# Attention: the fp16 halves of the probabilities cut by ScalarE and GpSimd and turned by DMA

## The reference, cut to what matters

```python
q = (layernorm(x) @ Wq)                      # per head, 64 wide
k, v = y @ Wkv                               # y: 1601 x 192 context
atten = softmax(einsum('bhid,bhjd->bhij', q, k) * SCALE, axis=-1)
res = einsum('bhij,bhjd->bhid', atten, v)
x = x + res @ Wproj + bproj
```

## Time and profile before

| | us |
|---|---|
| Median of three runs | 3374.56 |
| The profiled execution | 3373.66 |
| Its span, first to last instruction | 3371.6 |
| TensorE busy in the span | 3077.0 (91%) |
| VectorE, ScalarE, GpSimd busy | 2115.1, 1776.3, 941.7 |
| Tile loop of the attention, first score to last `X` addition | 85.4 to 2551.0 |

### The profile page before, as it was taken

One profiled execution on the slowest core, in us unless ns is written; L12 is line 12 of the kernel. 1 busy time (PEld: TensorE's weight loads), 2 busy tenths in 40 slices (PEclk: granted clock), 3 DMA queues, 4 the chain that ended last, 5 costly groups with the idle time before them and its releaser, 6 DMA issues. The chain is left out here.

```text
span 3371.6 us, 72486 instructions
## 1 busy us (share of the span) xinstructions
PE 3077.0 (91%) x27524; PEld 2053.9 (61%) x27524; DVE 2115.1 (63%) x4407; ACT 1776.3 (53%) x3522; POOL 941.7 (28%) x1018
## 2 busy tenths in 40 slices
PE   4999999999999999999999999999996557768998
PEld 3666667666766666676667667666764221145665
DVE  4666566656666665656565665656564659945665
ACT  2545454545455454545454454545453658815665
POOL 2141222222221322222222313222200238825553
PEclk8999999999999999999999999999998779988999
DMA  4111111111111211111111102111002000002111
GB/s 149 35 60 34 47 35 35 35 36 35 35 37 35 60 35 46 35 35 35 36 35 35 44 27 68 33 40 35 16 1 71 0 10 1 1 22 65 55 57 46
DMA packets 70375, 131.29 MB, mean 39 GB/s; under 512 B 6800, under 2 KB 52496, under 8 KB 69744
## 3 DMA queue, kind: packets, MB, share of 16 engines
q1 hardware_dynamic: 70000, 126.23, 12.9%
HBM read 122.02 MB, written 4.19 MB: 37 GB/s over the span
## 5 line engine op out<-in xcount | busy, mean ns | idle before, releaser
L428 PE MATMUL psum<-yT,Q 128*128 128x512 f16 (+1 forms) x5120 | 982.5, 333 | 14.5 <-issue 13.0
L452 PE MATMUL psum<-yN,pT 128*128 128x384 f16 (+1 forms) x3328 | 836.5, 326 | 0.0
L454 PE MATMUL psum<-yN,pT 128*128 128x192 f16 (+1 forms) x3328 | 815.1, 246 | 0.0
L645 DVE TENSOR_TENSOR pT<-psum,pT 128x512 f16<-128x512 f32 (+1 forms) x1024 | 578.6, 587 | 262.8 <-ACT pT L555 248.4
L555 ACT ACTIVATE pT<-psum 128x512 f16<-128x512 f32 (+1 forms) x1024 | 498.7, 514 | 433.0 <-PE psum L440 431.1
L428 PEld LDWEIGHTS psum<-yT,Q 128*128 128x128 f16 x5120 | 448.1, 98 | 384.7 <-issue 18.5
L338 POOL CAST yT<-stage 128x1601 f16<-128x1601 f32 x32 | 48.7, 1522 | 1825.7 <-DVE On L670 1785.5
L633 DVE TENSOR_REDUCE mx<-psum 128x1 f32<-128x1024 f32 (+1 forms) x512 | 481.9, 978 | 50.9 <-PE psum L428 32.2
L440 PE MATMUL psum<-ident,prob 128*128 128x128 f32 (+1 forms) x3328 | 502.2, 277 | 10.9 <-ACT prob L547 10.5
L547 ACT ACTIVATE prob<-psum,nb 128x1601 f32<-128x1601 f32 x256 | 408.6, 1596 | 194.7 <-DVE nb L637 194.7
L440 PEld LDWEIGHTS psum<-ident,prob 128*128 128x128 f32 (+1 forms) x3328 | 362.8, 140 | 150.3 <-DVE pT L645 93.4
(11 more groups left out here) (162 smaller groups left out, 3785.3 us busy)
## 6 DMA issues: line engine op xcount, KB each, us to landing
stage<-in_ctxT SPq DMA_DIRECT2D x32, 800.5 KB, 4.3
stage<-in_ctxT SPq DMA_DIRECT2D x64, 400.2 KB
stage<-in_ctxN SPq DMA_DIRECT2D x32, 672.0 KB, 3.9
wnat<-in_WF SPq DMA_DIRECT2D x32, 512.0 KB, 4.2
stage<-in_ctxN SPq DMA_DIRECT2D x32, 480.0 KB
X<-in_x SPq DMA_DIRECT2D x1, 2048.0 KB, 8.2
Wk<-in_WkS SPq DMA_DIRECT2D x1, 2048.0 KB, 16.4
x_rows<-X SPq DMA_DIRECT2D x1, 2048.0 KB, 8.2
```

The lines of the kernel that those rows point to most:

```text
L428: ins = pe.matmul(psS[:, lo:hi], Q[u][:, q, b, tt * P:(tt + 1) * P], yT[b][:, y, lo:hi], start=(n == 0), stop=(n == 4))
L452: pe.matmul(psO[:, 0:2 * CTX], pT[0][0:k, n, :], yN[b][0:k, n, :], start=(n == 0), stop=False)
L454: ins = pe.matmul(psO[:, 0:CTX], pT[1][0:k, n, :], yN[b][0:k, n, 0:CTX], start=False, stop=(n == JN - 1))
L645: dve.tensor_tensor(pT[1][0:w, lo:hi, :], psT[g % 2][0:w, 0:(hi - lo) * P].rearrange("p (n h) -> p n h", h=P), pT[0][0:w, lo:hi, :], ALU.s ...
```

## The change

The attention's tile loop is rewritten; the arithmetic is the same apart from where the halves are cut.

- The 13 transposes on TensorE, ScalarE's four PSUM copies and VectorE's four subtractions of a tile are gone. ScalarE casts `prob` to fp16 in one instruction (`ph`), GpSimd subtracts it (`pl`), and SyncE issues two DMA transposes per tile, SBUF to SBUF: `ph` to `hT` and `pl` to `lT`, both 128x1664 fp16. `ph` and `pl` have one buffer each, `hT` and `lT` two.
- The gather of a tile is two steps behind its scores (`BEHIND = 2`), `turn_o` three steps behind.
- The loops are unrolled over all 256 tiles. The projection is spread: one batch of nine matmuls in each of the steps `t` = 12 to 15 and, of the pair before, `t` = 0 to 3. It has a PSUM bank of its own.
- The context comes in eight pieces per batch element through three smaller staging buffers, one piece cut and one loaded per tile.

```diff
-        stage = [sb(f"stage{i}", [P, J]) for i in range(2)]
+        JH = 801
+        PIECES, RING = 8, 3
+        stage = [sb(f"stage{i}", [P, JH]) for i in range(RING)]
-        pT = [sb(f"pT{i}", [P, JN, P], F16) for i in range(2)]
+        ph = sb("ph", [P, JN * P], F16)
+        pl = sb("pl", [P, JN * P], F16)
+        hT = [sb(f"hT{i}", [P, JN, P], F16) for i in range(2)]
+        lT = [sb(f"lT{i}", [P, JN, P], F16) for i in range(2)]
...
+        # SyncE
+            for K in range(PIECES + 2):
+                load(K)
+            sp.wait_ge(pad_set, 2)
+            for G in range(NT):
+                if G >= 2:
+                    sp.wait_ge(summed, G - 1)
+                sp.wait_ge(hi_kept, G + 1)
+                sp.dma_start_transpose(hT[G % 2][:, :, :], ph[:, :]).then_inc(hi_turned, 16)
+                sp.wait_ge(lo_kept, G + 1)
+                sp.dma_start_transpose(lT[G % 2][:, :, :], pl[:, :]).then_inc(lo_turned, 16)
+                if G + PIECES + 2 < B * PIECES:
+                    load(G + PIECES + 2)
...
+        # GpSimd
+            for K in range(PIECES + 1):
+                cut(K)
+            for G in range(NT):
+                pool.wait_ge(hi_kept, G + 1)
+                if G:
+                    pool.wait_ge(lo_turned, 16 * G)
+                pool.tensor_tensor(pl[:, 0:J], prob[:, :], ph[:, 0:J], ALU.subtract).then_inc(lo_kept, 1)
+                if G + PIECES + 1 < B * PIECES:
+                    cut(G + PIECES + 1)
...
+            def gather(G):
+                b = G // HP % 2
+                if G:
+                    pe.wait_ge(normed, G)
+                pe.wait_ge(hi_turned, 16 * (G + 1))
+                pe.wait_ge(lo_turned, 16 * (G + 1))
...
+            # TensorE
+            for G in range(NT + BEHIND + 2):
+                p, t = divmod(G, 16)
+                if G < NT:
+                    score(G)
+                if BEHIND + 1 <= G < NT + BEHIND + 1:
+                    turn_o(G - BEHIND - 1)
+                if BEHIND <= G < NT + BEHIND:
+                    gather(G - BEHIND)
+                if t >= 12 and G < NT:
+                    project(p, t - 12)
+                if t < 4 and p:
+                    project(p - 1, t + 4)
+                # t < 2: q_half of the next pair; 2 <= t < 10: qk_group
...
+            def exponentials(G):
+                act.wait_ge(biased, G + 1)
+                if G:
+                    act.wait_ge(lo_kept, G)
+                act.activation(prob[:, :], psS[:, 0:J], ACT.Exp, bias=nb[:, G % 2:G % 2 + 1], scale=SCALE,
+                               accum_out=den[:, G % 4:G % 4 + 1]).then_inc(expd, 1)
+
+            def high(G):
+                act.wait_ge(expd, G + 1)
+                if G:
+                    act.wait_ge(hi_turned, 16 * G)
+                act.activation(ph[:, 0:J], prob[:, :], ACT.Copy).then_inc(hi_kept, 1)
...
+            # ScalarE, each step: exponentials(G), high(G), o_copy(G-3), sum_low(G-2), q_copy or qk_high
+            # VectorE, each step: maximum(G), reciprocal(G), o_low(G-3), normalise(G-2), q_low or qk_low,
+            #                     at t == 4 the addition of the pair before to X
```

More of the change, by code:

```diff
@@ L290, in attention, with place, transfers, loaded_by @@
         x_added = sem("x_added")
-        AHEAD, LO_AHEAD, CTX_AHEAD = 16, 4, 2
-        GROUPS = [(0, 4), (4, 8), (8, 12), (12, 13)]
+        NT = 16 * NPAIR
+        BEHIND = 2
+        def place(G):
+            p, t = divmod(G, 16)
+            b, tt = divmod(t, HP)
+            return p, t, b, tt
+        def transfers(part):
+            return 2 if part in (2, 3) else 1
+        def loaded_by(K):
+            return 16 * sum(transfers(k % PIECES) for k in range(K % RING, K + 1, RING))
+        def half_cols(part):
+            return slice(0, JH) if part % 2 == 0 else slice(JH, J)
@@ L371, in _, with q_half @@
+            for K in range(PIECES + 1):
[7 more added lines that the diff above has]
+                    cut(G + PIECES + 1)
         @block.tensor
         def _(pe):
-            def q_half(pair, half, misc_free):
-                misc_free()
+            def q_half(pair, half):
@@ L395, in qk_group, with score @@
                 ins.then_inc(qk_done, 1)
[L397 to L402, removed]
+            def score(G):
+                p, t, b, tt = place(G)
+                if tt == 0:
+                    pe.wait_ge(piece_cut, PIECES * (G // HP + 1))
+                if t == 0:
+                    pe.wait_ge(qk_lo, HP * (p + 1))
+                if G:
+                    pe.wait_ge(expd, G)
+                for c in range(4):
+                    lo, hi = 512 * c, min(J, 512 * (c + 1))
+                    for n, (q, y) in enumerate([(0, 0), (1, 1), (0, 2), (2, 0), (3, 1)]):
+                        ins = pe.matmul(psS[:, lo:hi], Q[p % 2][:, q, b, tt * P:(tt + 1) * P],
+                                        yT[b][:, y, lo:hi], start=(n == 0), stop=(n == 4))
+                    if c in (1, 3):
+                        ins.then_inc(scored, 1)
@@ new lines, in gather @@
+            def gather(G):
[4 more added lines that the diff above has]
+                pe.wait_ge(lo_turned, 16 * (G + 1))
+                for n in range(JN):
+                    k = P if n < JT else JR
+                    pe.matmul(psO[:, 0:2 * CTX], hT[G % 2][0:k, n, :], yN[b][0:k, n, :], start=(n == 0), stop=False)
+                    ins = pe.matmul(psO[:, 0:CTX], lT[G % 2][0:k, n, :], yN[b][0:k, n, 0:CTX], start=False, stop=(n == JN - 1))
+                ins.then_inc(summed, 1)
@@ new lines, in turn_o, with project @@
+            def turn_o(G):
+                pe.wait_ge(normed, G + 1)
+                if G:
+                    pe.wait_ge(o_kept, G)
+                for k in range(2):
+                    ins = pe.transpose(psT[:, k * P:(k + 1) * P], On[:, k * P:(k + 1) * P], ident[:, :])
+                ins.then_inc(o_turned, 1)
+            def project(p, tt):
+                pe.wait_ge(o_kept, 16 * p + HP + tt + 1)
+                if tt == 0 and p:
+                    pe.wait_ge(x_added, p)
+                for n, k in enumerate((2 * tt, 2 * tt + 1, H + tt)):
+                    for m, (o, w) in enumerate([(0, 0), (0, 1), (1, 0)]):
+                        ins = pe.matmul(psP, OT[:, o, k, :], Wvp[:, w, k, :], start=(tt == 0 and n == m == 0),
+                                        stop=(tt == HP - 1 and n == m == 2))
+                ins.then_inc(projected, 1)
@@ new lines, in _ @@
+                if g:
+                    pe.wait_ge(qk_lo, g)
+                qk_group(g)
+            for G in range(NT + BEHIND + 2):
+                p, t = divmod(G, 16)
+                if G < NT:
[8 more added lines that the diff above has]
+                    project(p - 1, t + 4)
+                if t < 10 and p + 1 < NPAIR:
+                    if t < 2:
+                        if t == 0:
+                            pe.wait_ge(qk_lo, HP * (p + 1))
+                        else:
+                            pe.wait_ge(q_kept, 2 * p + 3)
+                        q_half(p + 1, t)
+                    else:
+                        if t == 2:
+                            pe.wait_ge(q_kept, 2 * p + 4)
+                        else:
+                            pe.wait_ge(qk_lo, HP * (p + 1) + t - 2)
+                        qk_group(t - 2)
@@ new lines, in _ @@
+            q_copy(0)
+            q_copy(1)
+            for g in range(HP):
+                qk_high(g)
+            for G in range(NT + BEHIND + 1):
+                p, t = divmod(G, 16)
+                if G < NT:
+                    exponentials(G)
+                    high(G)
+                if BEHIND + 1 <= G:
+                    o_copy(G - BEHIND - 1)
+                if BEHIND <= G < NT + BEHIND:
+                    sum_low(G - BEHIND)
+                if t < 10 and p + 1 < NPAIR:
+                    if t < 2:
+                        q_copy(2 * p + 2 + t)
+                    else:
+                        qk_high(HP * (p + 1) + t - 2)
@@ new lines, in maximum @@
+            def maximum(G):
+                m = 2 * (G % 2)
+                for n, (lo, hi) in enumerate([(0, 1024), (1024, J)]):
+                    dve.wait_ge(scored, 2 * G + n + 1)
+                    dve.tensor_reduce(mx[:, m + n:m + n + 1], psS[:, lo:hi], AX_X, ALU.max).then_inc(maxed, 1)
+                dve.wait_ge(maxed, 2 * G + 2)
+                dve.tensor_scalar(nb[:, G % 2:G % 2 + 1], mx[:, m:m + 1], mx[:, m + 1:m + 2], -SCALE,
+                                  ALU.max, ALU.mult).then_inc(biased, 1)
@@ new lines, in _ @@
+            dve.memset(ph[:, J:], 0.0).then_inc(pad_set, 1)
+            dve.memset(pl[:, J:], 0.0).then_inc(pad_set, 1)
+            q_low(0)
+            q_low(1)
+            for g in range(HP):
+                qk_low(g)
+            for G in range(NT + BEHIND + 3):
+                p, t = divmod(G, 16)
+                if G < NT:
+                    maximum(G)
```

(13 more changed lines are left out.)

412 lines of the change are left out of this document (107 added, 305 removed).

## The result

The changed kernel takes 2960.56 us (median of four runs, 2959.42 to 2961.37), the kernel before 3375.95 us beside it. The ratio is 0.877, with a 95% interval of 0.875 to 0.878: 415 us less.

The account below looks back on a forecast made before the run. TensorE's own instructions, 98% busy in the tile loop, were taken as the bound. Each tile takes the longest of three loops: 132.6 us a pair, stage 2127 us, 338 less than 2465.6, so 3036 us; range 2940 to 3950.

Parts of the forecast that it names:

- The bound and what goes: Tile loop: TensorE's own instructions bind, 98% busy; 1.55 us a tile of transposes and short waits go from it.
- the 10 us of the last pair: Last pair of the stage: it forms no next queries, so 10 us less than the other pairs.
- What comes: New work per tile: ScalarE's cast 1.50 us, GpSimd's subtraction 3.22, a DMA transpose 4.3 to landing.
- the low bound: DMA transpose priced as a plain transfer of 426 KB: about 3.2 us to landing.
- The high bound of 12.6 us: DMA transpose priced as 1664 packets of 256 bytes at 99 ns each over 16 engines: 12.6 us to landing.
- The loops: Three loops run from tile to tile: `pl` 7.6 us, ScalarE-VectorE queues 7.38 or 8.15, TensorE 6.83 plus additions; the longest counts.
- the `pl` loop: GpSimd's next subtraction waits for the low half's landing: 3.22 + 4.3 + 0.1 of handovers, 7.6 us a tile.
- the chain: ScalarE and VectorE in-order queues, from one exponential to the next: 7.38 us, 8.15 with a `qk_group`.
- The slack: In front of the exponential: GpSimd's subtraction of the tile before is done 0.9 us before VectorE lets the exponential start.
- TensorE as the only bound: Rival, tile loop: each tile takes TensorE's own time, 126.7 us a pair, 2942 us in all; chance 0.08.
- The transposes setting the pace: Rival, tile loop: landing over 6.3 us makes the kernel slower, 3817 us at 8 us, about 6200 at 12.6; chance 0.34.

Follow-up runs that it names:

- e4_dummy: The changed kernel with 13 fp32 transposes of the identity, read by nothing, added on TensorE ahead of each tile's scores: 3290.62 us.
- e6_unroll: The kernel before with its attention loops unrolled on all five engines, nothing else changed: 3346.01 us against 3373.34 beside it.
- e8_nolow: The changed kernel without the low half's transpose and GpSimd's wait for it; the gather reads `hT` in place of `lT`: 2960.70 us.
- e1_order: The changed kernel with ScalarE copying tile G-3's turned output before tile G's exponential, and VectorE doing `o_low` before the reciprocal: 2925.91 us.
- e7_third: The changed kernel with a third transpose per tile, the high half into a spare buffer, and two staging buffers in place of three: 3092.86 us.

## Why the prediction was right, and where it was 75 us off

*The bound and what goes* held. The transposes' time on TensorE was paid out, 330 us by e4_dummy, and 27 more came from the turns of the loop (e6_unroll). No run shows the other 58 us by themselves, but the traces place them. In the order before, with turns between the scores, a tile takes 9.05 or 8.37 us where e4_dummy, with the same work in one block, takes 8.93 or 8.25: 0.12 a tile, some 29 us. A pair takes 152.1 us in e6_unroll and 148.9 in e4_dummy, which leaves about 22 us for the pairs' ends, where the projection stood alone. And the kernel before forms a 17th set of queries that nothing reads. The counts of TensorE's instructions on the two pages differ by 3456: 3328 transposes and 128 matmuls of that set, 9 us by the earlier trace rows. Together that is about 60. The set is one thing that the change took away besides what the section on it names. The forecast had the first two in its comparison of 154.1 with 132.6 us a pair, without naming them, and the third among the 10 us of the last pair.

*What comes* held for the cast and the subtraction. The transpose landed in 3.4 us, where 4.3 was taken and 3.2 was the low bound. The high bound of 12.6 us erred in the price of a packet. The count was nearly right: the queue has 952688 packets in the changed kernel and 518512 in e8_nolow, which is 1696 per transpose against 1664. But one takes 2.2x16/1696 = 0.021 us and not the 0.099 of the mean packet before.

The estimate from the Trainium skill's "DMA: Bandwidth & Descriptors", section "Latency and other measured facts", was 1.6 us of moving, at the 261 GB/s stated there; the 2.2 us worked out above are 194 GB/s. The estimate of 17 us, from the Trainium skill's "VectorE: DVE Perf Modes", section "The three transpose paths", took the time stated there for one block 13 times; 13 blocks in one instruction landed in 3.4 us, so that price can't be multiplied by the number of blocks.

*The loops* were the right ones, and each tile took the longest, but for three tiles: at `t` = 10 and 11 the forecast let the `pl` loop bind and at `t` = 12 TensorE, and it was the chain. The sum was too large by these terms, per pair:

- the chain of ScalarE and VectorE, 7.38 forecast and 7.16 measured, 8.15 and 7.83 with a `qk_group`. Back-to-back instructions of one engine overlap by some 0.1 us in the records: the next start after `o_low`'s and after `normalise`'s is earlier than the sum of durations, and the five handovers of 0.04 were mostly within the durations. Five tiles at 0.32 are 1.6 us.
- `pl`: 7.6 forecast, 3.23+3.4+0.1 = 6.7 with the measured landing, so it binds nowhere. With the chain, 0.9 us in the tiles of 7.16 before the projection.
- the first projection tile goes by the chain (7.16 for 7.85), the next is 7.72: 0.9 us.
- the addition to `X`: 8.16 for 8.57, 0.4; a `q_half` 1.75 us by starts for the 1.95 of its duration, 0.4 in two tiles.

These are 4.2 of the 4.3 us between 132.6 and 128.3, 69 us over 16 pairs. The loop was 73.5 us shorter than forecast; the rest lies at its two ends. The first pair took 120.4 us, since no projection of a pair before it runs in it, and the forecast gave it 132.6 like the others. The end after the last exponential's start at 2120.48 fits: from its end 1.68 later to 2138.6 it is 16.4 us, 16 forecast.

*The slack* in front of the exponential was there in nearly every tile, but in the tiles of 7.16 it was smaller than the 0.9 us forecast. In the tile shown above the subtraction ends at 1079.59 and the bias at 1080.15: 0.56 us. With a `qk_group` it is 1.22. VectorE ended 827.4 us of the waits in front of the exponential and GpSimd the other 29.7 us. The forecast's busy share of about 90% for TensorE doesn't follow from its own sum, in which 126.7 of 132.6 us, 96%, are TensorE's; 99% was measured.

*What was luck.* The transpose had no row, and the landing taken for it was the one term that nothing in the trace tied down. It came out 0.2 us above the low bound. A landing of 5.4 us, 2 more than measured, would by the forecast's own rule have made the `pl` loop 8.7 us, longer than TensorE's time in 14 of a pair's 16 tiles.

*The rivals.* TensorE as the only bound, 2942 us with a chance of 0.08, missed by 19 us, and the measured time lies nearer to it than to the forecast. What the forecast held against it, the written order of ScalarE's and VectorE's work, was the whole of the difference: e1_order takes the copies of `OT` and `o_low` out of the chain and reaches 2926. The transposes setting the pace, the largest rival with 0.34, was a fear of an unknown duration; e7_third shows that this kernel had room for two a tile and not for three.

## What to carry to other kernels

Where one engine is at 98% and is its own bound, work moved off it is paid out nearly in full (330 of 366 us here), and the next bound is found by writing each single-buffered loop and each in-order chain as a sum of rows and comparing it with that engine's own sum tile by tile. After such a change look for the idle time in front of the instruction that the chain releases: work that is ready by then belongs in it (35 us here for the order of two calls). A second buffer is worth nothing where its wait ends before a bound that has work queued, and a transfer that is only half hidden costs TensorE twice, once in the wait and once in the clock after it.

## What the runs showed of the hardware

- A DMA transpose of 128x1664 fp16 from SBUF to SBUF takes 3.4 us from issue to landing, holds the sixteen engines for about 2.2 us (an estimate from the DMA shares of 0.41 and 0.68) and SyncE's queue for 1.44 us. With two of them per 8.0 us and the loads the DMA share is 0.68; with two staging buffers in place of three it is 0.76 and a landing 3.8 to 3.9 us, and a third transpose brings it to 1.04 and 4.3 to 4.6.
- 63 of the 512 landings took over 4 us, up to 5.7; beside one that took 5.2 the issue rows are longer too (1.68 us in place of 0.59 for a load, 2.08 in place of 1.44 for a transpose). What causes it stays open.
- Idle stretches of TensorE of about 3.4 us in every second tile, in a stage in which it is busy 85% of the time, were followed in 96 of 128 cases by matmuls at half rate, at a granted clock of 0.52 in the one looked at and 0.93 over the stage. Doing useless transposes in that stretch brought the clock to 1.00 and made the kernel 106 us faster.
- Turns of the long loops: TensorE idles about 2 us twice at each of them with no releaser in the trace, and unrolling the loops made the kernel before 27 us faster.
